# Gate weights of the two best experts from one tanh instead of a softmax over eight

## The chip, the cores and the metric

The kernel runs on one core of a Trainium2 chip. A core has five engines, each with its own instruction stream: TensorE (PE in the profile; its weight loads are PEld), VectorE (DVE), ScalarE (ACT), GpSimd (POOL) and SyncE (SP, which here only starts DMAs). They meet through semaphores. The metric is the device time of one execution in microseconds; lower is better.

## The reference

The input has 16 batches of 768 tokens with 128 channels. Each batch goes through attention with eight heads, then through a mixture of eight experts of which every token uses two weights:

```
logits = x @ Wg                                   # eight per token
probs = softmax(logits)
top_p, _ = top_k(probs, 2)
top_p = top_p / sum(top_p)                        # two weights per token
for i in range(2):
    h = gelu(einsum(x * top_p[..., i:i+1], W1) + b1)   # all eight experts
    out = out + einsum(h, W2) + b2_sum
```

Every expert is computed for both weights; only the weights come from the gate. After the renormalisation the two weights are e1/(e1+e2) and e2/(e1+e2), with e1 and e2 the exponentials of the two largest logits.

## The kernel before

Everything is fp32. One round works on one batch. The feed-forward part of a round is 64 "units" (two chunks of 384 tokens, eight experts, four column blocks). The attention part of the next batch is cut into steps, and a table (PLAN) says in which of the 64 slots each step is issued, so that attention of batch b+1 runs between the units of batch b. In slot k each engine issues the attention steps of that slot, then unit k+4, then on TensorE the second product of unit k. There are 15 such rounds in a loop and one last round without a following batch; the attention of batch 0 stands ahead of the loop by itself.

A unit goes: TensorE forms z in PSUM in three products (lines 901 to 903, function `unit`); VectorE multiplies z by the ratio of the two weights into h1 (line 735); ScalarE applies gelu to z and to h1 (lines 540 and 541); GpSimd adds the two into hsum (line 453); TensorE multiplies hsum by W2 (line 912). TensorE's z has two buffers: unit m waits (line 897) until the gelu of line 540 of unit m-2 is done.

The end of the attention part prepares the expert input of the next batch, in slots 50 to 60:

- stats, seed, root, scale: layer norm on VectorE; line 627 is one of its small instructions, line 648 the six multiplies that form xn.
- turn (slot 56), gate (slot 57): TensorE transposes xn and forms the logits (line 879). VectorE takes the eight sorted logits of each of six token tiles (line 691) and subtracts the largest (line 694); ScalarE applies exp (line 524).
- weigh (slot 58): VectorE makes the two weights (`top`) and their ratio in eight instructions on 6 to 48 elements (lines 698 to 707), each waiting for the one before, and then scales xn by the larger weight in six multiplies of 128x128 (line 709).
- split (slot 60): TensorE transposes xn and the ratio (lines 886, 887); ScalarE and VectorE make x0_hi, ratio_b and x0_lo (lines 531, 532, 714). Unit 64, which is the first unit of the next batch, waits on TensorE for line 714.

In the gate slot ScalarE issues the gate's activation between the gelus of unit 60 and those of unit 61. After slots 58 and 59 VectorE goes on with the layer norm of the batch after next (lines 619 to 648). On ScalarE a table load (ACT_TABLE_LOAD) stands ahead of an activation whose function is not in the table set that is loaded.

Of the kernel before, what the change touches and what calls it, by code (L numbers as in the profile page):

```python
# [1 line left out]

# [7 lines left out]
ALU = mybir.AluOpType  # L24
ACT = mybir.ActivationFunctionType
AX = mybir.AxisListType

P = 128
# [60 lines left out]
WPB = len(WIDE) // 2  # L89
NPB = len(NARROW)  # L90

VCHAIN = 2 * (5 + 3 * NEWTON) + 7
NH1 = 4


# [20 lines left out]
def build(nc, x, Wq, Wk, Wv, Wo, time_bias, part_bias, Wg, W1, b1, W2, b2, out):  # L116
    with ExitStack() as ctx:
# [6 lines left out]
        def sem(name):  # L124
# [37 lines left out]
        ln_i = sb("ln_i", [P, TILES], I32)  # L162
        ln_y = sb("ln_y", [P, TILES])
        ln_t = sb("ln_t", [P, TILES])
        sorted_l, shifted, gate_e = (halves[:, 3, QCOLS + 48 * n:QCOLS + 48 * (n + 1)].rearrange(
            "p (i e) -> p i e", e=EXPERTS) for n in range(3))
        gate_s = sb("gate_s", [P, TILES, 4])
        probs = sb("probs", [P, TILES, 2])
        top = sb("top", [P, TILES, 2])
        ratio = sb("ratio", [P, TILES, 2])  # L170

# [305 lines left out]
        def _(act):  # L477
# [7 lines left out]
            def attention(r, step, a):  # L485
                if step in WIDE_STEPS:
                    s, _, filled = wide_at(r, step, a)
                    w = wide[s]
                if step == "turn":
                    act.wait_ge(wide_filled[s], filled)  # L490
                    act.copy(act_t[:, :], w[:, 0:TOK]).then_inc(wide_free[s], 1)
                elif step in ("query", "key"):
                    n, scale = (0, HD ** -0.5) if step == "query" else (2, 1.0)
                    act.wait_ge(wide_filled[s], filled)
                    act.activation(halves[:, n, :].bitcast(F32R), w[:, 0:TOK], ACT.Copy, scale=scale).then_inc(high_ready, 1)
                elif step == "value":
                    act.wait_ge(wide_filled[s], filled)
                    act.copy(val[:, :, :, 0:HD], w[:, 0:TOK].rearrange("p (i h d) -> p i h d", h=HEADS, d=HD)
                             ).then_inc(wide_free[s], 1)
                elif step == "rows":  # L500
                    act.wait_ge(wide_filled[s], filled)
                    act.activation(max_rows[:, 0, :].bitcast(F32R), w[0:GH * TILES, 0:P], ACT.Copy,
                                   scale=-1.0).then_inc(rows_high, 1)
                elif step == "scores":
                    g, hh, part = a
                    act.wait_ge(wide_filled[s], filled)
                    if not (g == 0 and isinstance(r.b, int) and r.b == 0) and hh == 0 and part == 0:

                        n = NARROW["mix", (1 - g, 1)]
                        act.wait_ge(narrow_filled, r.at(NPB, n + 1 - (NPB if g == 0 else 0)))  # L510
                    z0, z1 = ((0, 896), (896, 1664), (1664, ZW))[part]
                    act.activation(z[:, hh, z0:z1], w[:, 0:z1 - z0], ACT.Exp).then_inc(wide_free[s], 1)  # L512
                elif step == "mix":
                    g, qc = a
                    n = NARROW[step, a]
                    cols = QCOLS if qc == 0 else TOK - QCOLS
                    act.wait_ge(narrow_filled, r.at(NPB, n + 1))
                    if g == 1:

                        act.wait_ge(*taken(r, "divide", 0))  # L520
                    act.copy(mixed[:, qc * QCOLS:qc * QCOLS + cols], narrow[:, 0:cols]).then_inc(narrow_free, 1)  # L521
                elif step == "gate":
                    act.wait_ge(gate_shifted, r.at(1, 1))
                    act.activation(gate_e[:, :, :], shifted[:, :, :], ACT.Exp).then_inc(gate_exped, 1)
                elif step == "split":
                    act.wait_ge(wide_filled[s], filled)
                    if not (isinstance(r.b, int) and r.b == 0):

                        act.wait_ge(z_filled, r.at(UNITS, (a + 1) * UNITS_PER_CHUNK - UNITS))
                        act.wait_ge(z1_ready, r.at(UNITS, (a + 1) * UNITS_PER_CHUNK - UNITS + 2))  # L530
                    act.copy(x0_hi[:, a * CT:(a + 1) * CT], w[:, 0:CT]).then_inc(split_high, 1)
                    act.copy(ratio_b[:, a * CT:(a + 1) * CT], w[:, 512:512 + CT]).then_inc(split_high, 1)
# [28 lines left out]
        def _(vec):  # L561
# [37 lines left out]
            def attention(r, step, a):  # L599
# [72 lines left out]
                elif step == "sums":  # L672
                    vec.wait_ge(wide_filled[s], filled)
                    vec.reciprocal(recip[:, :, :], w[:, 0:TILES * GH].rearrange("p (i g) -> p i g", g=GH)).then_inc(wide_free[s], 1)
                elif step == "divide":
                    vec.wait_ge(wide_filled[s], filled)
                    if a == 1:

                        for hh in range(GH):
                            vec.wait_ge(stack_loaded[hh], r.at(2 * 4 * 16, 2 * 4 * 16))  # L680
                    vec.tensor_tensor(mixed_n[a][:, 0:TOK], mixed[:, :], w[:, 0:TOK], ALU.mult).then_inc(wide_free[s], 1)
                elif step == "project":
                    vec.wait_ge(wide_filled[s], filled)
                    vec.tensor_tensor(xs[:, :, :], w[:, 0:TOK].rearrange("p (i c) -> p i c", c=C),
                                      x_in[:, :, :], ALU.add).then_inc(wide_free[s], 1)
                elif step == "gate":
                    n = NARROW[step, a]
                    vec.wait_ge(narrow_filled, r.at(NPB, n + 1))
                    vec.sem_inc(vec_met, 1)
                    for i in range(TILES):  # L690
                        ins = vec.max(sorted_l[:, i, :], narrow[:, i * EXPERTS:(i + 1) * EXPERTS])
                    ins.then_inc(narrow_free, 1)
                    vec.wait_ge(narrow_free, r.at(NPB, n + 1))
                    vec.tensor_tensor(shifted[:, :, :], sorted_l[:, :, :], window(sorted_l[:, 0, :], 0, [[EXPERTS, TILES], [0, EXPERTS]]),
                                      ALU.subtract).then_inc(gate_shifted, 1)
                elif step == "weigh":
                    vec.wait_ge(gate_exped, r.at(1, 1))
                    vec.wait_ge(vec_chain, link(vec.tensor_reduce(gate_s[:, :, 0], gate_e[:, :, :], AX.X, ALU.add)))
                    vec.wait_ge(vec_chain, link(vec.reciprocal(gate_s[:, :, 1], gate_s[:, :, 0])))
                    vec.wait_ge(vec_chain, link(vec.tensor_tensor(probs[:, :, :], gate_e[:, :, 0:2],  # L700
                                                                  window(gate_s[:, 0, :], 1, [[4, TILES], [0, 2]]), ALU.mult)))
                    vec.wait_ge(vec_chain, link(vec.tensor_reduce(gate_s[:, :, 2], probs[:, :, :], AX.X, ALU.add)))
                    vec.wait_ge(vec_chain, link(vec.reciprocal(gate_s[:, :, 3], gate_s[:, :, 2])))
                    vec.wait_ge(vec_chain, link(vec.tensor_tensor(top[:, :, :], probs[:, :, :],
                                                                  window(gate_s[:, 0, :], 3, [[4, TILES], [0, 2]]), ALU.mult)))
                    vec.wait_ge(vec_chain, link(vec.reciprocal(ratio[:, :, 0], top[:, :, 0])))
                    vec.tensor_tensor(ratio[:, :, 1], top[:, :, 1], ratio[:, :, 0], ALU.mult)
                    for i in range(TILES):
                        ins = vec.tensor_scalar(xn[:, i, :], xn[:, i, :], top[:, i, 0:1], None, ALU.mult)
                    ins.then_inc(xn_ready, 1)  # L710
                    assert chain[0] == VCHAIN
                elif step == "split":
                    vec.wait_ge(split_high, r.at(4, 2 * a + 2))
                    ins = vec.tensor_tensor(x0_lo[:, a * CT:(a + 1) * CT], w[:, 0:CT], x0_hi[:, a * CT:(a + 1) * CT],
                                            ALU.subtract)
                    ins.then_inc(wide_free[s], 1)
                    if not (isinstance(r.b, int) and r.b == 0) and a == 0:
                        vec.wait_ge(out_ready, r.at(CHUNKS, 1 - CHUNKS + 1))
                    if a == 0:
                        residual(r, 0)  # L720
                    elif isinstance(r.b, int) and r.b == 0:
                        residual(r, 1)
# [219 lines left out]
```

## Time and profile before

| what | value |
|---|---|
| median of three timed executions | 2823.3 us (2819.64 to 2824.63) |
| span of the profiled execution, first to last instruction | 2817.5 us |
| what lies around the span (median less span) | 5.8 us |
| TensorE busy | 2460.9 us (87%) |
| weight loads busy | 2132.1 us (76%) |
| VectorE busy | 1485.6 us (53%) |
| ScalarE busy | 1694.7 us (60%) |
| GpSimd busy | 1087.3 us (39%) |
| mean granted clock of TensorE | 0.965 |

The profile gives the span of the profiled execution; its time from outside was not recorded apart, so the median of the timed ones stands for it. Busy shares are means over stages with different limits. In timelines a row begins with its start in microseconds and its length; "x6" merges six instructions, and "[0.97 <-ACT h L540]" is idle time of that engine just before, with what ended it.

### The profile page before, as it was taken

Reading aid. Unit: us, or ns where it says so; the run is one execution under the profiler, and the core shown is the slowest. Engines: PE = TensorE matmul, PEld = TensorE weight load, DVE = VectorE, ACT = ScalarE, POOL = GpSimd, SP = SyncE. Lnnn points to the kernel's source line nnn. Section 1 sums busy time; section 2 is a strip of 40 time slices with the busy share of each in tenths; the row PEclk is TensorE's granted clock in tenths of the full one; section 3 lists DMA queues with packets and bytes.
Section 4 is the critical chain, followed back from the end, with each engine's and each line's share of the span. In section 5 each row is a group of like instructions: output and inputs, shape, how many; then the busy total and the mean of one; then the engine's idle time right before and its main releaser. Section 6 shows DMA issues by size and latency. Waiting matters only on the chain.

```text
span 2817.5 us, 57193 instructions
## 1 busy us (share of the span) xinstructions
PE 2460.9 (87%) x18611; PEld 2132.1 (76%) x18611; DVE 1485.6 (53%) x4157; ACT 1694.7 (60%) x2788; POOL 1087.3 (39%) x1054
## 2 busy tenths in 40 slices
PE   1658989899998989989899898989989898998989
PEld 0447778787877878877787777878877787877879
DVE  7545375445636554474554636544573555547454
ACT  2126666665665666556566665666566566656667
POOL 6014244343424434343343424333343433434337
PEclk9679999999999999999999999999999999999999
DMA  2412121030212203021030212103021120302100
GB/s 32 71 37 29 22 33 27 10 47 10 27 27 30 29 7 49 6 32 27 12 46 9 29 25 32 27 8 48 10 27 27 25 35 7 43 11 32 27 9 7
DMA packets 62290, 73.55 MB, mean 26 GB/s; under 512 B 15936, under 2 KB 43488, under 8 KB 61920
## 3 DMA queue, kind: packets, MB, share of 16 engines
q1 hardware_dynamic: 62016, 69.89, 17.1%
q8 instruction: 173, 2.83, 0.4%
q14 instruction: 101, 0.83, 0.1%
HBM read 11.19 MB, written 6.29 MB: 6 GB/s over the span
## 4 chain that ended last, share of the span: by engine, by line
PE 65%; DVE 12%; issue 10%; ACT 8%; DMA 2%; POOL 1%; SPq 1%; DVEq 0%; POOLq 0%; ACTq 0%
PE acc L912 17%; PE zps L901 8%; PE wide L819 7%; PE narrow L852 5%; PE wide L835 5%; ACT z L512 5%; PE zps L902 5%; PE zps L903 5%; PE wide L838 4%; PE wide L866 2%; PE wide L873 2%; DVE wide L664 1%; DVE h L735 1%; PE wide L859 1%; DMA stack<-halves 1%
## 5 line engine op out<-in xcount | busy, mean ns | idle before, releaser
L453 POOL TENSOR_TENSOR hsum<-h 128x384 f32<-128x384 f32 x1024 | 1027.6, 1007 | 1575.0 <-ACT h L541 1507.3
L540 ACT ACTIVATE h<-zps,b_col 128x384 f32<-128x384 f32 x1024 | 594.2, 580 | 751.6 <-DVE h L735 728.3
L735 DVE TENSOR_TENSOR h<-zps,ratio_b 128x384 f32<-128x384 f32 x1024 | 562.1, 554 | 910.1 <-PE zps L903 906.1
L912 PE MATMUL acc<-w,hsum 128*128 128x128 f32 x6144 | 863.0, 277 | 1.4 <-DVE outt L744 1.2
L912 PEld LDWEIGHTS acc<-w,hsum 128*128 128x128 f32 x6144 | 845.8, 194 | 2.2 <-POOL hsum L453 1.7
L541 ACT ACTIVATE h<-h,b_col 128x384 f32<-128x384 f32 x1024 | 620.4, 606 | 0.0
L901 PE MATMUL zps<-x_hi,w_lo 128*128 128x384 f32 x1024 | 449.8, 439 | 105.8 <-ACT h L540 64.0
L664 DVE CUSTOM_DVE_ANT_0 wide<-wide,query_table 128x768 f32<-128x768 f32 (+5 forms) x768 | 463.0, 651 | 123.1 <-PE wide L819 117.3
L835 PE MATMUL wide<-stack 128*128 128x256 f32 (+3 forms) x1280 | 364.7, 317 | 71.8 <-ACT z L512 33.6
L512 ACT ACTIVATE z<-wide 128x896 f32<-128x896 f32 (+2 forms) x384 | 344.8, 918 | 87.3 <-PE wide L838 86.8
L902 PE MATMUL zps<-x_lo,w_hi 128*128 128x384 f32 x1024 | 352.5, 344 | 0.0
L903 PE MATMUL zps<-x_hi,w_hi 128*128 128x384 f32 x1024 | 351.7, 343 | 0.0
L901 PEld LDWEIGHTS zps<-x_hi,w_lo 128*128 128x128 f32 x1024 | 197.4, 193 | 191.8 <-issue 100.3
L838 PE MATMUL wide<-bias_rows,key_hot 128*128 128x256 f32 (+3 forms) x1280 | 340.5, 300 | 0.0
L835 PEld LDWEIGHTS wide<-stack 128*128 128x128 f32 x1280 | 244.9, 191 | 124.9 <-ACT z L512 77.6
L819 PE MATMUL wide<-stack 64*128 64x512 f32 (+3 forms) x1024 | 260.8, 364 | 17.2 <-DVE maxes L664 8.6
L838 PEld LDWEIGHTS wide<-bias_rows,key_hot 128*128 128x128 f32 x1280 | 245.8, 192 | 6.4
L819 PEld LDWEIGHTS wide<-stack 64*128 64x128 f32 x1024 | 164.0, 191 | 76.7 <-DVE maxes L664 13.4
L902 PEld LDWEIGHTS zps<-x_lo,w_hi 128*128 128x128 f32 x1024 | 199.4, 195 | 0.4
L903 PEld LDWEIGHTS zps<-x_hi,w_hi 128*128 128x128 f32 x1024 | 196.8, 192 | 0.0
L852 PE MATMUL narrow<-z,val 128*32 128x256 f32 (+3 forms) x2560 | 175.9, 393 | 3.5 <-ACT mixed L521 1.4
L852 PEld LDWEIGHTS narrow<-z,val 128*32 128x32 f32 x2560 | 83.0, 109 | 87.5 <-issue 21.8
(110 smaller groups left out, 1611.8 us busy)
## 6 DMA issues: line engine op xcount, KB each, us to landing
stack<-halves SPq DMA_DIRECT2D x512, 96.0 KB, 3.6
x_in<-in_x SPq DMA_DIRECT2D x136, 48.0 KB, 2.4
out_dram<-outt SPq DMA_DIRECT2D x256, 24.0 KB, 1.6
z<-in_L_ffn_W SPq DMA_DIRECT2D x8, 256.0 KB, 4.2
stack<-max_rows SPq DMA_DIRECT2D x64, 12.0 KB
bias_rows<-w_hi SPq DMA_DIRECT2D x1, 192.0 KB
bias_rows<-w SPq DMA_DIRECT2D x1, 192.0 KB
bias_rows<-w_lo SPq DMA_DIRECT2D x1, 192.0 KB
```

Of the source, the lines that this page charges most:

```text
L453: pool.tensor_tensor(hsum[:, m % NHS, :], h0[:, m % 2, :], h1[:, m % NH1, :], ALU.add).then_inc(hsum_ready, 1)
L540: act.activation(h0[:, m % 2, :], zps[m % 2][:, 0:CT], ACT.Gelu, bias=b1_col[:, j:j + 1]).then_inc(h0_ready, 1)
L541: act.activation(h1[:, m % NH1, :], h1[:, m % NH1, :], ACT.Gelu, bias=b1_col[:, j:j + 1]).then_inc(h1_ready, 1)
L664: ins = vec.tensor_tensor_reduce(w[:, at:at + n], w[:, at:at + n], query_table[:, h, TOK - n:TOK], 1.0, -3e38, ALU.add, ALU.max, maxes[:, ...
L735: vec.tensor_tensor(h1[:, m % NH1, :], zps[m % 2][:, 0:CT], ratio_b[:, c * CT:(c + 1) * CT], ALU.mult).then_inc(z1_ready, 1)
L819: ins = pe.matmul(w[:, at:at + k1 - k0], qst[0:64, hh, i * P:(i + 1) * P], kst[0:64, hh, k0:k1], start=True, stop=True)
L835: pe.matmul(w[:, at:at + q1 - q0], kst[:, hh, i * P:(i + 1) * P], qst[:, hh, q0:q1], start=True, stop=False)
L838: ins = pe.matmul(w[:, at:at + q1 - q0], key_hot[:, g, :], bias_rows[:, hh, q0 - i * P:q1 - i * P], start=False, stop=True)
L901: pe.matmul(zp, lo, x0_hi[:, cols], start=True, stop=False)
L902: pe.matmul(zp, hi, x0_lo[:, cols], start=False, stop=False)
L903: pe.matmul(zp, hi, x0_hi[:, cols], start=False, stop=True).then_inc(z_filled, 1)
L912: ins = pe.matmul(acc[:, n * P:(n + 1) * P], hsum[:, k % NHS, n * P:(n + 1) * P], w2[:, j, :], start=(j == 0 and n == 0), stop=(j == UNITS ...
```

## The change

The subtraction of the gate step now forms only d, the second logit taken from the first (one value per token, 6 per partition). ScalarE computes t = tanh(d/2). VectorE forms the weights as (1+t)/2 and (1-t)/2, then the reciprocal of the first and the ratio. Three small buffers are new, four are gone, and the count of chained VectorE instructions per round (VCHAIN) is five lower. The lines of the new kernel carry numbers that are 14 lower up to line 680 and 21 lower after the weigh step.

```diff
-VCHAIN = 2 * (5 + 3 * NEWTON) + 7
+VCHAIN = 2 * (5 + 3 * NEWTON) + 2
@@ buffers
-        sorted_l, shifted, gate_e = (halves[:, 3, QCOLS + 48 * n:QCOLS + 48 * (n + 1)].rearrange(
-            "p (i e) -> p i e", e=EXPERTS) for n in range(3))
-        gate_s = sb("gate_s", [P, TILES, 4])
-        probs = sb("probs", [P, TILES, 2])
+        sorted_l = halves[:, 3, QCOLS:QCOLS + 48].rearrange("p (i e) -> p i e", e=EXPERTS)
+        gate_d = sb("gate_d", [P, TILES])
+        gate_t = sb("gate_t", [P, TILES])
+        gate_r = sb("gate_r", [P, TILES])
@@ ScalarE, gate
-                    act.activation(gate_e[:, :, :], shifted[:, :, :], ACT.Exp).then_inc(gate_exped, 1)
+                    act.activation(gate_t[:, :], gate_d[:, :], ACT.Tanh, scale=0.5).then_inc(gate_exped, 1)
@@ VectorE, gate
-                    vec.tensor_tensor(shifted[:, :, :], sorted_l[:, :, :], window(sorted_l[:, 0, :], 0, [[EXPERTS, TILES], [0, EXPERTS]]),
-                                      ALU.subtract).then_inc(gate_shifted, 1)
+                    vec.tensor_tensor(gate_d[:, :], sorted_l[:, :, 0], sorted_l[:, :, 1], ALU.subtract).then_inc(gate_shifted, 1)
@@ VectorE, weigh
-                    vec.wait_ge(vec_chain, link(vec.tensor_reduce(gate_s[:, :, 0], gate_e[:, :, :], AX.X, ALU.add)))
-                    vec.wait_ge(vec_chain, link(vec.reciprocal(gate_s[:, :, 1], gate_s[:, :, 0])))
-                    vec.wait_ge(vec_chain, link(vec.tensor_tensor(probs[:, :, :], gate_e[:, :, 0:2],
-                                                                  window(gate_s[:, 0, :], 1, [[4, TILES], [0, 2]]), ALU.mult)))
-                    vec.wait_ge(vec_chain, link(vec.tensor_reduce(gate_s[:, :, 2], probs[:, :, :], AX.X, ALU.add)))
-                    vec.wait_ge(vec_chain, link(vec.reciprocal(gate_s[:, :, 3], gate_s[:, :, 2])))
-                    vec.wait_ge(vec_chain, link(vec.tensor_tensor(top[:, :, :], probs[:, :, :],
-                                                                  window(gate_s[:, 0, :], 3, [[4, TILES], [0, 2]]), ALU.mult)))
-                    vec.wait_ge(vec_chain, link(vec.reciprocal(ratio[:, :, 0], top[:, :, 0])))
-                    vec.tensor_tensor(ratio[:, :, 1], top[:, :, 1], ratio[:, :, 0], ALU.mult)
+                    vec.tensor_scalar(top[:, :, 1], gate_t[:, :], -0.5, 0.5, ALU.mult, ALU.add)
+                    vec.wait_ge(vec_chain, link(vec.tensor_scalar(top[:, :, 0], gate_t[:, :], 0.5, 0.5, ALU.mult, ALU.add)))
+                    vec.wait_ge(vec_chain, link(vec.reciprocal(gate_r[:, :], top[:, :, 0])))
+                    vec.tensor_tensor(ratio[:, :, 1], top[:, :, 1], gate_r[:, :], ALU.mult)
```

ScalarE in the loop, from the gelus of unit 60 to those of unit 61 (line 540 and 541), before the change; line 524 is the gate's activation:

```order
L540 ACTIVATE h<-zps,b_col 128x384
L541 ACTIVATE h<-h,b_col 128x384
L523 REGISTER_ALU
L524 ACT_TABLE_LOAD
L524 ACTIVATE halves<-halves 128x48
L537 REGISTER_ALU
L540 ACT_TABLE_LOAD
L540 ACTIVATE h<-zps,b_col 128x384
L541 ACTIVATE h<-h,b_col 128x384
```

The same place after the change, where the gelus are lines 526 and 527 and the gate's activation is line 510:

```order
L526 ACTIVATE h<-zps,b_col 128x384
L527 ACTIVATE h<-h,b_col 128x384
L509 REGISTER_ALU
L510 ACTIVATE gate_t<-gate_d 128x6
L523 REGISTER_ALU
L526 ACTIVATE h<-zps,b_col 128x384
L527 ACTIVATE h<-h,b_col 128x384
```

Two table loads are gone, one ahead of the gate's activation and one ahead of the gelu behind it; no other instruction of ScalarE moved. In the attention of batch 0, ahead of the loop, no table load stood at line 524, and none is gone there.

VectorE in the loop, from the gate's subtraction to the six multiplies, before the change (register instructions left out; line 735 is unit 61):

```order
L694 TENSOR_TENSOR halves<-halves 128x48
L735 TENSOR_TENSOR h<-zps,ratio_b 128x384
L698 TENSOR_REDUCE gate_s<-halves 128x6
L699 RECIPROCAL gate_s<-gate_s 128x6
L700 TENSOR_TENSOR probs<-halves,gate_s 128x12
L702 TENSOR_REDUCE gate_s<-probs 128x6
L703 RECIPROCAL gate_s<-gate_s 128x6
L704 TENSOR_TENSOR top<-probs,gate_s 128x12
L706 RECIPROCAL ratio<-top 128x6
L707 TENSOR_TENSOR ratio<-top,ratio 128x6
L709 TENSOR_SCALAR xn<-xn,top 128x128 x6
```

And after it (line 714 is unit 61, line 688 the six multiplies):

```order
L680 TENSOR_TENSOR gate_d<-halves 128x6
L714 TENSOR_TENSOR h<-zps,ratio_b 128x384
L683 TENSOR_SCALAR top<-gate_t 128x6
L684 TENSOR_SCALAR top<-gate_t 128x6
L685 RECIPROCAL gate_r<-top 128x6
L686 TENSOR_TENSOR ratio<-top,gate_r 128x6
L688 TENSOR_SCALAR xn<-xn,top 128x128 x6
```

Eight small instructions became four, in the same place of the stream. TensorE, GpSimd and SyncE have the same instructions in the same order as before.

## Rows read from the trace of the kernel before

**Rows 1.** The page: span and the busiest engine (busy us, share, instructions).
```profile
span 2817.5 us, 57193 instructions
PE 2460.9 (87%) x18611; PEld 2132.1 (76%) x18611; DVE 1485.6 (53%) x4157; ACT 1694.7 (60%) x2788; POOL 1087.3 (39%) x1054
```

**Rows 2.** Groups by line, ScalarE's table loads: count | busy us, mean ns | idle before.
```profile
L540 ACT ACT_TABLE_LOAD x46 | 59.0, 1283 | 24.3 <-DVE h L735 22.1
...
L524 ACT ACT_TABLE_LOAD x15 | 19.2, 1283 | 0.3
```

**Rows 3.** Waits, whole span: engine line waited for: us, times, longest.
```profile
ACT h L540 <- DVE h L735: 728.3, 591, 3.0
...
PE zps L901 <- ACT h L540: 64.0, 59, 8.4
...
PE zps L901 <- DVE x_lo L714: 41.8, 16, 2.8
```

**Rows 4.** Timeline of ScalarE around the last gate in the loop.
```profile
2718.21 0.60 ACT L541 ACTIVATE h<-h,b_col 128x384 f32<-128x384 f32 x1
2718.83 1.28 ACT L524 ACT_TABLE_LOAD   x1
2720.12 0.24 ACT L524 ACTIVATE halves<-halves 128x48 f32<-128x48 f32 x1
2720.61 1.28 ACT L540 ACT_TABLE_LOAD   x1 [0.24 <-DVE h L735]
2721.90 0.58 ACT L540 ACTIVATE h<-zps,b_col 128x384 f32<-128x384 f32 x1
```

**Rows 5.** Timeline of VectorE, same place.
```profile
2719.80 0.21 DVE L694 TENSOR_TENSOR halves<-halves 128x48 f32<-128x48 f32 x1
2719.97 0.56 DVE L735 TENSOR_TENSOR h<-zps,ratio_b 128x384 f32<-128x384 f32 x1
2720.45 0.20 DVE L698 TENSOR_REDUCE gate_s<-halves 128x6 f32<-128x48 f32 x1
...
2722.05 1.26 DVE L709 TENSOR_SCALAR xn<-xn,top 128x128 f32<-128x128 f32 x6
2723.23 1.02 DVE L735 TENSOR_TENSOR h<-zps,ratio_b 128x384 f32<-128x384 f32 x2
...
2726.10 0.93 DVE L627 TENSOR_SCALAR ln_v<-moments 128x6 f32<-128x6 f32 x1
```

**Rows 6.** Timeline of TensorE: units 63, 64 and 67.
```profile
2722.54 0.45 PE L901 MATMUL zps<-x_hi,w_lo 128*128 128x384 f32 x1 [0.97 <-ACT h L540]
...
2728.06 0.44 PE L901 MATMUL zps<-x_hi,w_lo 128*128 128x384 f32 x1 [2.75 <-DVE x_lo L714]
...
2733.21 0.44 PE L901 MATMUL zps<-x_hi,w_lo 128*128 128x384 f32 x1 [1.31 <-ACT h L540]
```

**Rows 7.** Timeline of GpSimd, same round.
```profile
2713.02 2.07 POOL L453 TENSOR_TENSOR hsum<-h 128x384 f32<-128x384 f32 x2 [0.63 <-ACT h L541]
...
2723.07 1.10 POOL L453 TENSOR_TENSOR hsum<-h 128x384 f32<-128x384 f32 x1 [3.17 <-ACT h L541]
2725.03 1.97 POOL L453 TENSOR_TENSOR hsum<-h 128x384 f32<-128x384 f32 x2 [0.86 <-ACT h L541]
```

**Rows 8.** Timeline of VectorE: line 648 ahead of the loop, and in the loop.
```profile
192.71 1.62 DVE L648 TENSOR_SCALAR xn<-xs,moments,ln_y 128x128 f32<-128x128 f32 x6
...
2712.18 3.00 DVE L648 TENSOR_SCALAR xn<-xs,moments,ln_y 128x128 f32<-128x128 f32 x6
```

**Rows 9.** Timeline of VectorE: batch 0's gate, ahead of the loop.
```profile
204.18 3.83 DVE L700 TENSOR_TENSOR probs<-halves,gate_s 128x12 f32<-128x12 f32 x1
...
208.98 1.26 DVE L709 TENSOR_SCALAR xn<-xn,top 128x128 f32<-128x128 f32 x6
```

**Rows 10.** Busy time from unit 64's start, two rounds: start:end length, engines (instructions), granted clock.
```profile
1555.30:1558.70 3.40, 3.34 (x13) 3.35 (x14) 2.71 (x11) 1.08 (x2) 0.27 (x1) 0.53 0.00 0
2728.00:2731.40 3.40, 3.34 (x24) 3.34 (x25) 3.14 (x11) 1.08 (x2) 0.70 (x1) 1.00 0.00 0
```

## Prediction

> **What bounds the kernel now.** I read the page first: TensorE is busy for 87% of 2817.5 us [rows 1], so a gain must come from TensorE's gaps, not from the busy time of the engine that is changed. Next the groups of ScalarE: 61 table loads at lines 524 and 540, 1283 ns each [rows 2]. Fifteen of them stand ahead of the gate's exp, and 15 of the 46 ahead of the gelu behind it; the code shown ahead says that these 30 go. They cost ScalarE 30 x 1.283 = 38.5 us. Then the waits: ScalarE itself waits 728 us for VectorE's line 735, so it has room; TensorE waits 64.0 us for ScalarE's gelu and 41.8 us for VectorE's x_lo, the latter 16 times, once a batch [rows 3]. So the question is which of the two is late at the gate.
>
> The timelines of the last gate in the loop answer it; all rounds of the loop look alike here, so one is worked out and multiplied by 15. ScalarE ends unit 60 at 2718.81, loads a table, runs exp at 2720.12, loads again at 2720.61 and starts unit 61's gelu at 2721.90 [rows 4]. TensorE misses that gelu: unit 63 starts at 2722.54 after a gap of 0.97. But its next stop is unit 64 at 2728.06, after a gap of 2.75 that VectorE's x_lo ends [rows 6]. VectorE has no gap between: subtraction 2719.80, unit 61 at 2719.97, the eight small instructions from 2720.45, the six multiplies from 2722.05, units 62 and 63 from 2723.23, then the next layer norm up to the split [rows 5]. A wait that is removed on TensorE before 2722.54 is therefore only moved into the gap before 2728.06. VectorE's chain bounds this place, and ScalarE's loads are beside it.
>
> **The change part by part.** All times are those of the round above.
>
> Table loads: exp's load covered the wait for the logits, and its successor can go at once. Without the second load unit 61's gelu starts at 2720.61, when its input is there, 1.29 earlier [rows 4]. TensorE's unit 63 moves up by its gap, 0.97, and waits at the split instead. Worth on the path: nothing.
>
> Tanh for exp: the input is ready when the subtraction ends, 2720.01; exp took 0.24 for 48 elements, and the new one has 6. It ends by 2720.3, before VectorE asks at 2720.45. Nothing on the path.
>
> Subtraction, 6 elements for 48: by rows 5, 0.56 for 384 elements and 0.21 for 48, an element costs about 1 ns, so 0.04 is saved. All that follows on VectorE moves by it.
>
> Weigh: eight instructions took 2722.05 - 2720.45 = 1.60, or 0.20 each. Of the four new ones the second does not wait for the first, and the multiplies don't wait for the fourth, as now. I count three steps, 0.60: a saving of 1.00. Bounds: four full steps, saving 0.80; and two and a half, 1.10.
>
> What takes it back: the six multiplies now start at 2721.05, and GpSimd's sum comes earlier too, because the gelu does. GpSimd's sum of unit 61 starts 1.17 after the gelu of line 540 (2723.07 less 2721.90 [rows 4, 7]); it will ask at 2721.78. The multiplies start every 0.20 (1.18 to the next unit, by six [rows 5]), so the fifth starts at 2721.84 and meets it. What such a meeting costs: the tiny line 627 at 2726.10 took 0.93 and ended at 2727.03, just after GpSimd's pair that ended at 2727.00; line 648 took 1.62 ahead of the loop where GpSimd was idle, and 3.00 in the loop beside a pair of sums [rows 5, 7, 8]. A multiply that meets a running sum stands until its end. Today the sum starts at 2723.07 during the sixth multiply, so GpSimd is the one that stands, 0.1. With a sum of 1.10 from 2721.78 the fifth multiply ends at about 2722.91 instead of 2722.12: 0.79 lost. Of 1.00 there remain 0.21. If the fifth gets in ahead of the sum, the sixth stands instead, with about the same result. Bounds: all of it lost, or nothing of it.
>
> [...]
>
> Behind the multiplies everything follows VectorE rigidly: units 62 and 63, their gelus, the pair of sums at 2725.03, line 627 that stands for that pair, x_lo, unit 64. So a round saves 0.04 + 0.21 = 0.25, and 15 rounds 3.75.
>
> Batch 0, ahead of the loop: line 700 stands until 208.01 for GpSimd's work on the weights, and the multiplies start at 208.98 [rows 9], 0.97 later. After the change the first small instruction will stand in its place until the same moment, and about 0.55 follow. Saves 0.4, once.
>
> Sum against the profiled execution: 2817.5 - 4.15 = 2813.4 of span, and with the 5.8 between span and median, 2823.3 - 4.15 = 2819.2. I forecast 2819.
>
> **The rivals.**
>
> First, the meeting does not happen or costs little: the multiplies slip past the sum. For it: the fifth and sixth multiply start within 0.25 of the sum, and my steps are good to 0.1 or so. Against: the whole chain is rigid and would have to be 0.25 faster. Price 1.04 a round, 15.6 + 0.4 = 16.0: 2807.
>
> Second, the other side: TensorE's clock. Today its idle time here is in two pieces, 0.97 and 2.75, with work between; after the change the first closes and the gap before unit 64 grows to some 3.2 to 3.5. [...] Against: two thirds of the idle time exists already, and most rounds keep the high clock here.
>
> Third, the loads stay, as the change doesn't do what it says. [...] The order of instructions shows none. Then the sum would come late as today and miss the multiplies, while unit 63 at 2722.54 would hold VectorE's second line 735, which could start about 0.8 later, 2723.3 instead of 2723.70: 0.4 a round, 2817.
>
> Fourth, ScalarE bounds after all: 2 x 1.283 x 15 = 38.5, 2785. The gap of 2.75 that x_lo ends, not a gelu, speaks against it.
>
> Fifth, something behind gives back even the quarter (a DMA or the clock elsewhere): 2823.
>
> **How the numbers follow.** Chances: forecast 0.52, first rival 0.20, second 0.14, third 0.04, fourth 0.03, fifth 0.07. The likeliest case has its own range of 2814 to 2823, from a lost saving to twice mine with the scatter of the timed runs. The 8 in 10 range runs from the first rival to the near part of the second: 2807 to 2830. A measurement of this kernel tells 0.2%, 5.6 us, from no change. Faster than 2817.7: the first and fourth rival, half of the third, and a third of the forecast: 0.40. Slower than 2828.9: two thirds of the second: 0.09. Within: 0.51.
>
> **What would show it.** In the profile after: 31 table loads at these two lines for 61; the gelu of unit 61 about 0.8 after the subtraction's start, not 2.1; the six multiplies starting some 1.3 after it and lasting about 2.1 instead of 1.26, with a sum of GpSimd beginning in their middle; unit 64 about 8.0 after the subtraction instead of 8.26; TensorE's wait for x_lo near 50 us, and that for the gelu lower by about 14. I am wrong if the multiplies keep 1.26 (first rival), if the granted clock falls near unit 64 in most rounds (second), or if unit 64 moves by over a microsecond.

## The result and the profile after

The changed kernel took 2805.6 us (median of 4 runs, 2798.97 to 2806.65) against 2822.1 for the kernel before on the same chip; the ratio is 0.9934 with a 95% interval of 0.992 to 0.9949. I had forecast 2819, a gain of 0.15%, with a range from 2807 to 2830. The gain was four times as large. A "round" below is the time from one gate subtraction to the next, averaged over 14 rounds of the loop in the profiled execution; "low" is the lower of the two clocks that the profiles record for TensorE, 0.50 of full speed (the other is 1.00, and a row with a value between them spans both), and a "low stretch" is a stretch of a few microseconds in which that clock was granted. The "turn of the loop" is the jump from the end of the loop's body back to its start; TensorE's first products behind it start 16 to 18 us after the subtraction. Rounds are counted from the first one of the loop.

The page of the kernel after, its first and third line, answering to [rows 1]:

```profile
span 2803.3 us, 57024 instructions
...
PE 2461.5 (88%) x18611; PEld 2135.8 (76%) x18611; DVE 1478.3 (53%) x4093; ACT 1651.6 (59%) x2758; POOL 1087.5 (39%) x1054
```

TensorE's work is the same. ScalarE lost 43 us of busy time, and the span shrank by only 14, which speaks against loads on the path; e1 and the pair f2 and f3 below decide it. Its groups, for [rows 2] (line 526 was 540):

```profile
L526 ACT ACT_TABLE_LOAD x31 | 39.8, 1283 | 20.0 <-DVE h L714 18.0
```

The 30 loads are gone. The waits, for [rows 3] (880 was 901, 693 was 714):

```profile
ACT h L526 <- DVE h L714: 750.1, 601, 3.0
...
PE zps L880 <- DVE x_lo L693: 48.0, 16, 3.2
...
PE zps L880 <- ACT h L526: 37.0, 35, 8.1
```

TensorE's wait for the gelu fell by 27 us, that for x_lo rose by 6. I had forecast 14 for the first: the gap of 0.97 ahead of unit 63 is gone in every round, 14.6 us, and the gap of 1.3 ahead of unit 67 is down to between 0.0 and 0.4 in 13 rounds of 14, where before it was down in 4. Those are the rounds in which unit 64 runs at the low clock, as the table below shows. The last gate in the loop, ScalarE, VectorE, GpSimd and TensorE one after the other, for [rows 4 to 7]; its subtraction starts at 2706.14:

```profile
2706.34 0.21 ACT L510 ACTIVATE gate_t<-gate_d 128x6 f32<-128x6 f32 x1 [1.50 <-DVE gate_d L680]
2706.96 0.58 ACT L526 ACTIVATE h<-zps,b_col 128x384 f32<-128x384 f32 x1 [0.41 <-DVE h L714]
```

```profile
2706.85 0.17 DVE L684 TENSOR_SCALAR top<-gate_t 128x6 f32<-128x6 f32 x1
2707.05 0.19 DVE L685 RECIPROCAL gate_r<-top 128x6 f32<-128x6 f32 x1
2707.28 0.17 DVE L686 TENSOR_TENSOR ratio<-top,gate_r 128x6 f32<-128x6 f32 x1
2707.36 2.00 DVE L688 TENSOR_SCALAR xn<-xn,top 128x128 f32<-128x128 f32 x6
2709.28 1.01 DVE L714 TENSOR_TENSOR h<-zps,ratio_b 128x384 f32<-128x384 f32 x2
```

```profile
2708.12 1.16 POOL L439 TENSOR_TENSOR hsum<-h 128x384 f32<-128x384 f32 x1 [2.21 <-ACT h L527]
```

```profile
2714.11 0.44 PE L880 MATMUL zps<-x_hi,w_lo 128*128 128x384 f32 x1 [3.17 <-DVE x_lo L693]
```

This is the forecast's picture: gelu at 0.82 after the subtraction, multiplies from 1.22, GpSimd's sum starting at 1.98, six multiplies in 2.00 instead of 1.26, unit 64 at 7.97 where it was at 8.26. One by one, the fifth multiply started at 2.01, 0.02 behind the sum, and still took its usual 0.28, while the sum took 1.16 for 1.00; the sixth, due at 2.20, stood until the sum ended and took 1.02. A round of the loop should then have lost 0.28. It lost 1.08: from 167.47 to 166.39 us.

Where the rest is shows in the granted clock. Busy time in stretches of 3 us, from unit 64's start and from the next batch's first transposes behind the turn of the loop. The columns are those of [rows 10]: start:end and length, then TensorE, its weight loads, VectorE, ScalarE and GpSimd with their instructions, then the granted clock, the DMA share and GB/s. The kernel before, the fifth round, 167.53 us long:

```profile
1051.60:1054.60 3.00, 3.00 (x22) 3.00 (x23) 2.74 (x11) 1.08 (x2) 0.41 (x1) 1.00 0.00 0
1060.70:1063.70 3.00, 3.00 (x14) 3.00 (x15) 0.56 (x1) 0.80 (x1) 0.68 (x1) 0.50 0.21 41
```

The kernel after, its fifth round (165.11 us) and its eighth (168.06 us):

```profile
1048.10:1051.10 3.00, 3.00 (x15) 3.00 (x16) 2.75 (x11) 1.08 (x2) 0.46 (x1) 0.66 0.00 0
1057.10:1060.10 3.00, 3.00 (x24) 3.00 (x25) 0.62 (x2) 0.80 (x1) 0.72 (x1) 1.00 0.21 42
1547.70:1550.70 3.00, 3.00 (x12) 3.00 (x13) 2.23 (x10) 1.07 (x2) 0.00 (x0) 0.50 0.00 0
1557.60:1560.60 3.00, 2.93 (x13) 2.94 (x13) 0.40 (x1) 0.80 (x1) 0.37 (x1) 0.50 0.22 44
```

Before, the usual round has the high clock at unit 64 and the low one behind the turn: 14 products are at work in those 3 us, where the fifth round after has 24. After, the low clock has come to unit 64 in nearly every round, and in half of them the stretch behind the turn is at full speed. Counted in the clock's record over 14 rounds, with all later runs (unit 64's place is the median of the 14; the runs are explained in the next section):

| kernel | unit 64 after the subtraction | round | low at unit 64 | low behind the turn | median us | ratio (95%) |
|---|---|---|---|---|---|---|
| before | 8.26 | 167.47 | 4 | 12 | 2822.1 | |
| changed | 7.98 | 166.39 | 13 | 7 | 2805.6 | 0.9934 (0.992 to 0.9949) |
| e1, loads kept | 7.54 | 165.94 | 11 | 9 | 2796.0 | 0.9921 (0.9904 to 0.9937) |
| e2, loads gone alone | 8.93 | 167.46 | 8 | 7 | 2821.0 | 1.0011 (1.0001 to 1.0021) |
| e3, one step more | 8.21 | 166.98 | 11 | 7 | 2814.1 | 0.998 (0.997 to 0.999) |
| f1, before, filling that missed | 8.27 | 169.42 | 0 | 14 | 2846.6 | 1.0097 (1.0076 to 1.0118) |
| f2, changed, filling that missed | 8.01 | 168.92 | 0 | 14 | 2840.4 | 1.0077 (1.006 to 1.0093) |
| f3, e1, filling that missed | 7.55 | 168.40 | 0 | 14 | 2830.6 | 1.0043 (1.0026 to 1.006) |
| g1, before, filled at 64 | 8.27 | 167.94 | 0 | 14 | 2824.2 | 1.001 (1.0 to 1.0019) |
| g2, changed, filled at 64 | 7.99 | 167.19 | 0 | 14 | 2814.8 | 0.9978 (0.9968 to 0.9987) |
| h1, before, filled at both | 8.27 | 166.07 | 0 | 0 | 2802.0 | 0.993 (0.9912 to 0.9948) |
| h2, changed, filled at both | 8.01 | 165.62 | 0 | 0 | 2791.9 | 0.9893 (0.9876 to 0.9911) |
| v1, multiplies first | 6.93 | 164.96 | 14 | 5 | 2784.5 | 0.9881 (0.9865 to 0.9898) |
| v2, v1 filled at the turn | 6.93 | 164.45 | 8 | 0 | 2776.2 | 0.9842 (0.9826 to 0.9859) |
| v3, v1 filled at both | 6.93 | 164.41 | 0 | 0 | 2773.5 | 0.9834 (0.9817 to 0.985) |

All ratios are to the kernel before on the same chip, whose median there was 2818.8 to 2823.9; so medians from different chips compare to some 5 us only. Ahead of batch 0's gate, where the kernels don't differ, the profiled executions are already up to 3 us apart (199.7 to 202.7). The runs e1 to e3 shared a chip, and so did f1 to f3 with v1, g1 and g2 with v2 and v3, and h1 with h2. Low stretches elsewhere in the round are not counted here: the kernel before has one 160 us after the subtraction in 5 rounds, h1 one at 159 in 4, and these rounds are no longer than the others. One place where it did matter comes with e3.

### The profile page after: what moved, and what is told of

The parts are those of the page before. It is cut to its first block, busy times and chain, and to the rows that moved or that the text cites. A ratio compares the mean times of both kernels' runs of the same rounds, so it can differ in the third digit from the quotient of the medians.

```text
span 2803.3 us, 57024 instructions
## 1 busy us (share of the span) xinstructions
PE 2461.5 (88%) x18611; PEld 2135.8 (76%) x18611; DVE 1478.3 (53%) x4093; ACT 1651.6 (59%) x2758; POOL 1087.5 (39%) x1054
## 4 chain that ended last, share of the span: by engine, by line
PE 69%; DVE 11%; issue 10%; ACT 8%; POOL 1%; DMA 0%; DVEq 0%; SPq 0%; POOLq 0%; ACTq 0%
PE acc L891 19%; PE zps L880 8%; PE wide L798 7%; PE narrow L831 6%; PE zps L882 5%; PE zps L881 5%; ACT z L498 5%; PE wide L814 5%; PE wide L817 4%; PE wide L845 2%; PE wide L852 2%; DVE h L714 2%; DVE wide L650 1%; PE wide L838 1%; PE wide L782 1%
```

## The experiments

Three theories stood. Local: only VectorE's way to unit 64 counts, with the meeting of the multiplies and GpSimd's sum. Clock: the rest of the gain is the place of the low stretches. Loads: the table loads were on the path after all. Where an edit changes the number of chained VectorE instructions, the count VCHAIN follows; that line is left out of the diffs shown.

**e1, the loads kept.** Unit 61's gelu comes late again while the chain stays short.

```diff
-act.activation(gate_t[:, :], gate_d[:, :], ACT.Tanh, scale=0.5)
+act.activation(gate_t[:, :], gate_d[:, :], ACT.Exp, scale=0.5)
```

> The changed kernel with exp in the place of tanh, so the two table loads of each round come back while VectorE's short chain stays (the weights it computes are not those of the reference). Local theory (only VectorE's way to unit 64 counts, and GpSimd's sum meets the multiplies only when the loads are gone): the six multiplies last 1.26 again, unit 64 starts 7.8 to 7.9 after the subtraction instead of 8.26 before and 8.0 in the changed kernel; 15 x 0.4 + 0.4 = 6 us below before, ratio 0.998. Clock theory (most of the change's gain comes from where TensorE's clock falls, and that depends on how its idle time is cut up): TensorE's idle time is cut as before (a gap of about 1 and one of 2.3), so the low stretches stay where they were before and the ratio is 0.998 as well; if instead the gain is the same as that of the change, 0.993, then loads and idle pieces have nothing to do with it. Rival that the loads were on the path: ratio 1.00 or more.

Measured: 2796.0, ratio 0.9921. VectorE, GpSimd and TensorE at the last gate, whose subtraction starts at 2697.30:

```profile
2698.52 1.26 DVE L688 TENSOR_SCALAR xn<-xn,top 128x128 f32<-128x128 f32 x6
```

```profile
2700.56 1.98 POOL L439 TENSOR_TENSOR hsum<-h 128x384 f32<-128x384 f32 x2 [3.49 <-ACT h L527]
```

```profile
2704.84 0.43 PE L880 MATMUL zps<-x_hi,w_lo 128*128 128x384 f32 x1 [2.04 <-DVE x_lo L693]
```

The multiplies are done before the sum starts and last 1.26; unit 64 is at 7.54, better than the 7.8 expected. Two loads a round are back, and the kernel is no slower than the change: 0.9921 and 0.9934 have overlapping intervals, and the same pair with filling on one chip (f2 and f3 below) has the kernel with the loads ahead by 9.8 us. The loads theory fails, and the meeting is shown. The time went further down than 0.998, for which the clock's part was again not foreseen (9 rounds of 14 low behind the turn, not 12).

**e2, the loads gone alone.** The kernel before, with

```diff
-window(sorted_l[:, 0, :], 0, [[EXPERTS, TILES], [0, EXPERTS]])
+window(sorted_l[:, 0, :], 7, [[EXPERTS, TILES], [0, EXPERTS]])
-act.activation(gate_e[:, :, :], shifted[:, :, :], ACT.Exp)
+act.activation(gate_e[:, :, :], shifted[:, :, :], ACT.Tanh)
```

> The kernel before with tanh in the place of exp, so only the two table loads go and the eight small instructions stay (the subtraction takes the smallest logit, to keep the values finite; the weights are not those of the reference). Local theory: GpSimd's sum now asks 1.98 after the subtraction's start, just ahead of the first multiply at 2.25, so VectorE stands until about 3.0 and unit 64 starts at about 9.0 instead of 8.26: 15 x 0.75 = 11 us slower, ratio 1.004. Rival that the loads were on the path: faster by up to 38 us, ratio 0.986. Clock theory: the gap of 0.97 is closed and the gap ahead of unit 64 is the longest of all, above 4, so the clock is low at unit 64 in nearly every round and less often at the next batch's first transposes; that gives some 10 us back, ratio near 1.000.

Measured: 2821.0, ratio 1.0011. VectorE and TensorE at the last gate, whose subtraction starts at 2721.22; GpSimd's sum ran from 2723.21 to 2724.20:

```profile
2723.39 0.83 DVE L707 TENSOR_TENSOR ratio<-top,ratio 128x6 f32<-128x6 f32 x1
2724.15 1.25 DVE L709 TENSOR_SCALAR xn<-xn,top 128x128 f32<-128x128 f32 x6
```

```profile
2730.15 0.44 PE L901 MATMUL zps<-x_hi,w_lo 128*128 128x384 f32 x1 [3.17 <-DVE x_lo L714]
```

The last small instruction, with two inputs in SBUF, stood for the sum and took 0.83 where it took 0.17, and unit 64 came at 8.93, 0.67 late. By the local theory alone this is +10 us. The kernel was slower by 3; 7 rounds were low behind the turn where 12 had been. Both halves of the expectation hold: removing the loads does harm at its place, and the clock pays most of it back.

**e3, one step more.** The changed kernel with line 685 issued twice, each waiting for the one before.

```diff
+vec.wait_ge(vec_chain, link(vec.reciprocal(gate_r[:, :], top[:, :, 0])))
 vec.wait_ge(vec_chain, link(vec.reciprocal(gate_r[:, :], top[:, :, 0])))
```

> The changed kernel with the reciprocal of the weigh step issued twice, one more chained small instruction of 0.2 us. Local theory: the multiplies start 0.2 later, GpSimd's sum stands where it was, so the fourth or fifth multiply waits for the same end and the two behind it come as before or one multiply (0.2) later; unit 64 at 8.0 to 8.2 after the subtraction. If the local quarter of a microsecond were all of the gain the time would go back to the kernel before, ratio 0.999 to 1.000. Clock theory: TensorE's idle time is cut as in the changed kernel, and the ratio stays near 0.993 to 0.995.

Measured: 2814.1, ratio 0.998, between the two expectations. Unit 64 is at 8.21, all but where it was before the change, so locally almost nothing is gained; the round is still 0.49 shorter than before, with 7 low stretches behind the turn where 12 had been. The 0.23 that unit 64 lost against the change cost 8.5 us in the medians (12 when each is taken against the kernel before on its own chip), not 3.5.

Yet e3 has as many low stretches behind the turn as the change, and two fewer at unit 64, so the two columns of the table don't explain its loss. The trace does in part: in three of its rounds (169.1 to 169.8 us) a third low stretch stands 121 us after the subtraction, at the products of line 815, behind a wait for a DMA that lasted 2.0 to 2.2 in these rounds and 1.2 to 1.4 in the others. The third round, and then the twelfth, which has the same two low stretches without the third and took 167.34:

```profile
829.85 0.50 PE L815 MATMUL wide<-stack 128*128 128x512 f32 x1 [2.23 <-DMA stack<-max_rows]
...
2331.07 0.50 PE L815 MATMUL wide<-stack 128*128 128x512 f32 x1 [1.37 <-DMA stack<-max_rows]
```

```profile
830.60:833.90 3.30, 3.30 (x16) 3.30 (x16) 0.00 (x0) 1.73 (x2) 0.00 (x0) 0.50 0.00 0
2331.80:2335.10 3.30, 3.16 (x23) 2.71 (x21) 0.00 (x0) 2.66 (x4) 0.08 (x1) 1.00 0.00 0
```

The three rounds lie 2.1 above that one, 0.45 a round over the 14, of the 0.59 by which e3's round is above the change's. Why the DMA came later there is open. The place of the low stretches moves with small shifts, and no fixed price can be put on it.

**f1 to f3, a filling that missed.** Products that nobody reads, to keep TensorE at work in its two long idle stretches, in the kernel before, the changed one and e1:

```diff
+if j == 0 and c == 0 and not isinstance(r.b, int):      # ahead of unit 64
+    pe.wait_ge(narrow_free, r.at(NPB, NARROW["gate", 0] + 1))
+    for _ in range(3):
+        pe.matmul(narrow[:, 0:448], ident[:, :], W448, start=True, stop=True)
...
+if a == 0 and not isinstance(r.b, int):                  # in turn, ahead of its wait
+    for _ in range(2):
+        pe.matmul(w[:, 0:448], ident[:, :], W448, start=True, stop=True)
```

W448 stands for the first 448 columns of w2.

> The kernel before with TensorE kept at work in its two longest idle stretches of a round: three products of 448 columns ahead of its wait for unit 64, two ahead of its wait for the first transposes of the next batch, into PSUM that is overwritten; nothing reads them. Clock theory: the low stretches near unit 64 and at the next transposes go or become rare, a round takes about 165 us or less for 167.5, and the time falls by 20 us or more although work was added: ratio 0.990 or lower. Rival (the low clock costs nothing, it only lies in slack): ratio 1.000 to 1.003, as the added products can only delay.

> The changed kernel with the same added products. Local theory with the clock held alike: unit 64 is 0.28 earlier than in f1_before_filled, and the difference between the two is 15 x 0.28 + 0.4 = 4.6 us, not the 16 measured without the products. If the change itself is worth the 16, this run is 16 below f1.

> The kernel of e1_loads_kept (short chain, exp, both table loads) with the same added products. Local theory: unit 64 is 0.72 earlier than in f1_before_filled: 15 x 0.72 + 0.4 = 11 us below it, and 6.5 us below f2_changed_filled. If the clock made the difference between e1 and the change, the two are alike here.

Measured: 2846.6, 2840.4 and 2830.6, ratios 1.0097, 1.0077 and 1.0043. f1's expectation failed. The products in turn ran behind the idle stretch, not in it: the stretch of 2.4 us there ends at the first transposes of the loop's body and is put down to "issue", so it is the turn of the loop, not the wait in turn. All rounds kept the low clock behind the turn in all three, and the differences shrank towards the local ones: 6.2 between f1 and f2 (4.6 expected, 16.5 without filling) and 16.0 between f1 and f3 (11 expected, 22.8 without filling).

**g1 and g2, filled ahead of unit 64 alone**, the first half of that edit.

> The kernel before with the three added products ahead of unit 64 alone. (In f1 to f3 the two products meant for the next transposes ran behind the gap there, which is the turn of the loop, and only cost time.) Clock theory as it now stands: idle time ahead of unit 64 brings a low stretch there, which is cheap because much of it lies in slack and which takes the place of the dear one behind the turn of the loop. With the products no low stretch comes at unit 64 and one comes behind the loop's turn in every round: a round takes 167.3 to 167.6, ratio 0.999 to 1.001. If low stretches at unit 64 were a pure loss, taking them away would make it faster: 0.998 or less.

> The changed kernel with the three added products ahead of unit 64. Clock theory: nearly every round now has the low stretch behind the loop's turn, as in the kernel before, a round takes 0.28 less than in g1, 167.1 or so; 2815 to 2819, ratio 0.998, so that taking idle time from TensorE makes the changed kernel 10 us slower. If the 16 us of the change were its own, the ratio stays near 0.993.

Measured: 2824.2 (1.001) and 2814.8 (0.9978), both ratios as expected; g1's round, 167.94, is 0.3 longer than expected. No low stretch at unit 64, one behind the turn in every round, and the changed kernel is 9 us slower than without the products (11 against the kernel before on each one's chip), although they fit into idle time and unit 64 starts where it did. The cheap low stretch had stood in for the dear one.

**v1, the multiplies first.** The changed kernel, with a chain of two small instructions:

```diff
-vec.tensor_scalar(top[:, :, 1], gate_t[:, :], -0.5, 0.5, ALU.mult, ALU.add)
 vec.wait_ge(vec_chain, link(vec.tensor_scalar(top[:, :, 0], gate_t[:, :], 0.5, 0.5, ALU.mult, ALU.add)))
-vec.wait_ge(vec_chain, link(vec.reciprocal(gate_r[:, :], top[:, :, 0])))
-vec.tensor_tensor(ratio[:, :, 1], top[:, :, 1], gate_r[:, :], ALU.mult)
+vec.reciprocal(ratio[:, :, 1], top[:, :, 0])
...
-act.copy(ratio_b[:, a * CT:(a + 1) * CT], w[:, 512:512 + CT])
+act.activation(ratio_b[:, a * CT:(a + 1) * CT], w[:, 512:512 + CT], ACT.Copy, bias=-1.0)
```

> A version of the change whose multiplies get away ahead of GpSimd's sum: only the larger weight is made from tanh, its reciprocal is written in the ratio's place (ratio = 1/larger - 1), and ScalarE takes the 1 off where it copies ratio_b anyway. Two small VectorE instructions are left of eight. Local theory: the multiplies start at 0.94 to 1.0 after the subtraction and the sixth at about 1.95, before the sum asks at 1.99; they last 1.26, and unit 64 starts at about 7.0 to 7.3 for 8.26 before: 15 x 1.1 = 16 us from this alone, and the time is at or below that of e1_loads_kept (2796). If the sixth meets the sum all the same: unit 64 at 7.9, 2806. The clock adds or takes up to 12 in either case.

Measured: 2784.5, ratio 0.9881. VectorE, GpSimd and TensorE at the last gate, whose subtraction starts at 2685.69:

```profile
2686.34 0.16 DVE L683 TENSOR_SCALAR top<-gate_t 128x6 f32<-128x6 f32 x1
2686.54 0.19 DVE L684 RECIPROCAL ratio<-top 128x6 f32<-128x6 f32 x1
2686.64 1.22 DVE L686 TENSOR_SCALAR xn<-xn,top 128x128 f32<-128x128 f32 x6
2687.78 1.01 DVE L712 TENSOR_TENSOR h<-zps,ratio_b 128x384 f32<-128x384 f32 x2
```

```profile
2687.68 1.05 POOL L439 TENSOR_TENSOR hsum<-h 128x384 f32<-128x384 f32 x1 [2.20 <-ACT h L527]
```

```profile
2692.62 0.44 PE L878 MATMUL zps<-x_hi,w_lo 128*128 128x384 f32 x1 [2.66 <-DVE x_lo L691]
```

The sixth multiply starts at 1.90, 0.09 ahead of the sum, so GpSimd stands for 0.05 and VectorE not at all. Unit 64 is at 6.93: 1.33 a round, of which the change as made got 0.28.

**v2 and v3, v1 with filling at the turn, and at both places.** Two products at the end of the loop's body (v2), and two ahead of unit 64 as well (v3):

```diff
+if k == UNITS - 1 and not isinstance(r.b, int):
+    pe.wait_ge(narrow_free, r.at(NPB, NPB + NARROW["gate", 0] + 1))
+    for _ in range(2):
+        pe.matmul(narrow[:, 0:448], ident[:, :], W448, start=True, stop=True)
```

> v1 with two added products of 448 columns at the end of the loop's body, ahead of the gap at the loop's turn. If the gap of 2.3 is the fetch of the first instructions of the body and TensorE can work meanwhile, the products cost little and the low stretch behind the turn (5 of 14 rounds in v1) goes: 5 x 1.9 = 10 us below v1, 2775. If the engine has to end them first, each round is 1.2 longer and what the clock gives is lost: 2790 to 2803.

> v2 with two added products ahead of unit 64 as well. Clock theory: a round without any low stretch. If v2's products are free: under 2770. If they cost 1.2 a round: 2780 to 2795. More low stretches than in v1 would say that the added products don't count as work for the clock.

Measured: 2776.2 (0.9842) and 2773.5 (0.9834). TensorE at a turn of the loop in v2:

```profile
2528.09 1.67 PE L895 MATMUL narrow<-w,ident 128*128 128x448 f32 x4
2530.70 0.87 PE L775 MATMUL wide<-ident,xn 128*128 128x128 f32 x6 [0.94 <-issue]
```

The engine worked 1.67 us of the turn and stood idle for 0.94 (0.9 to 1.4 over v2's rounds); the kernel before stood 2.39 at its turn in the fifth round. The products are almost free, and no round was low behind the turn any more. v2 met its expectation (2775); v3 missed its "under 2770", as a low stretch at unit 64 is cheap. Most of it lies in the gap ahead of unit 67, which in v2 was 1.3 in each round without one and 0.0 to 0.4 in each round with one; in v2 rounds with one took 164.61 on average (8), and rounds without one 164.22 (6). v3's fifth round, the same two places as above, both at the high clock:

```profile
1039.20:1042.20 3.00, 2.99 (x21) 3.00 (x22) 2.74 (x11) 1.08 (x2) 0.36 (x1) 1.00 0.00 0
1048.60:1051.60 3.00, 2.98 (x23) 2.99 (x24) 0.91 (x2) 1.29 (x3) 0.43 (x1) 1.00 0.17 33
```

v3 is the fastest version that was run, 1.7% below the kernel before; v1 needs no added work and is 1.2% below it.

**h1 and h2, both kernels filled at both places**, three products ahead of unit 64 and two at the turn.

> The kernel before with three added products ahead of unit 64 and two ahead of the loop's turn, as v3. Clock theory: neither of the two low stretches is left, and rounds differ from those of v3 only by where unit 64 starts (8.26 against 6.93): 164.4 + 1.33 = 165.7 a round, 2773.5 + 15 x 1.33 + 0.5 = 2794, ratio 0.990. If the two low stretches were not what made the kernel before slow, it stays above 2810.

> The changed kernel with the same added products. With the clock high in both kernels the change is worth its own part only, 15 x 0.28 + 0.4 = 4.6 us: 2789, 0.16% below h1. If the change's 16 us were its own and not the clock's, this run is 16 below h1, 2778.

Measured: 2802.0 (0.993) and 2791.9 (0.9893). Neither has a low stretch at the two places in any round. Filling alone makes the kernel before 0.7% faster, about as much as the change did. Between the two, the change is worth 10.1 us in the medians and 0.45 a round (6.8 us in 15): more than my 4.6, less than the 16.5 without filling. Both expected medians were too low, by 8 and 3.

## Why the prediction was wrong

Local steps. The loads off the path, right: TensorE got its 0.97 and waited longer at x_lo, and e1, with the loads, is no slower than the change. Tanh hidden, right: 0.21 us, ended before VectorE asked. The chain, right: 1.03 shorter to the multiplies' start, forecast 1.04. The meeting with GpSimd, right: 0.74 lost, forecast 0.79; the fifth multiply got in and the sixth stood, the variant that the forecast named with the same result. Unit 64 came 0.28 earlier, forecast 0.25. Batch 0's multiplies came 0.56 earlier after their subtraction, forecast 0.4. The 5.8 between span and median is not what lies around the span: for one and the same execution of the changed kernel that is 1.8 (2805.14 less 2803.3), so the profiled execution of the kernel before was itself some 4 us faster than its median. The forecast difference doesn't rest on it. A small instruction with two SBUF inputs stood for a sum as well: in e2 line 707 took 0.83, where it took 0.17 in the kernel before.

What failed is one step: "So a round saves 0.04 + 0.21 = 0.25, and 15 rounds 3.75", with "all rounds of the loop look alike here" behind it. It takes the other 157 us of a round as fixed; the measured saving was 1.08 a round. They are not fixed: a round with the low clock behind the turn of the loop is longer than one without. In the changed kernel the rounds with a low stretch at unit 64 alone took 165.49 on average (7 rounds), those with one at both places 167.37 (6): 1.9. Taking all of these stretches away took 1.6 a round off from g2 to h2 and 1.9 from g1 to h1. The change went from 12 to 7 such stretches in 14 rounds, 8 to 10 us by these prices.

The first rival's number, 2807, is close to the 2805.6 measured by luck: its sign, multiplies that keep 1.26, did not come (2.00). The second rival, TensorE's clock, was right in what happens and had the wrong sign. It had the gap before unit 64 grow and the low clock come there, as a loss. Both came: 3.17 us of idle where there had been 2.75, and 13 low rounds where there had been 4; with the gap filled (g1 and g2) there was none. The upper end of the range, 2830, rests on a price for this rival that was an estimate of mine and that no run shows; what v2 showed is about 0.4 a round, as most of it lies in the slack ahead of unit 67. What I did not ask is where the low stretch had been that it replaced. The rows for that were in the trace before: the first transposes behind the turn of the loop at half speed in 12 rounds of 14, and none of the three views I read shows it, as the engine counts as busy there.

How much is whose. Three pairs hold the clock's places alike in both kernels: the change is worth 6.2 us between f1 and f2 and 9.4 between g1 and g2 (all rounds low behind the turn), and 10.1 between h1 and h2 (none). So of the measured 16.5 us some 6 to 10 are its own, and the rest came from the clock, which g2 (9 us slower with idle time removed) and h1 (0.7% faster) show from both sides.

That own part is more than the 4.6 us of unit 64, and the waits show one more piece that the prediction lacked. In h1, at unit 76 in every second round, TensorE waits for a DMA into `stack`:

```profile
PE wide L819 <- DMA stack<-halves: 2.1, 8, 0.3
```

The row is there with 2.1 to 2.3 us in all five kernels with the old gate (before, e2, f1, g1, h1) and in none of the ten with the new one. The lead of h2 over h1 grows by 0.18 between units 72 and 80, where it lies, and so do v3's lead over h1 and g2's over g1. Why the old gate has this wait no run isolates.

Open are the other pieces. The lead of h2 over h1 is 0.27 at units 64 to 67, 0.09 behind the turn (units 68 to 72), 0.26 at unit 80 and 0.42 at unit 120; between h1 and v3 the round shrinks by 1.66 where unit 64 explains 1.33. And which rounds will be low behind the turn, or elsewhere as in e3, I cannot work out beforehand. Medians of this kernel are the sum of a small sure part and a part that depends on this.

## What to carry to other kernels

Before a saving is multiplied by the number of rounds, look at TensorE's granted clock round by round, in stretches of a few microseconds behind each of its idle stretches; a change of a quarter of a microsecond can move where it runs at half speed (here 0.28 at unit 64, and low behind the turn in 7 rounds of 14 where 12 had been). An engine that is released earlier starts its next instruction earlier, and on VectorE and GpSimd that instruction may now meet one of the other engine: give each edit both partners' start times, as here, where two dropped table loads by themselves made unit 64 0.67 us later. When small instructions stand ahead of large ones, issue first what the large ones need, and move the rest behind or onto an engine that touches the data anyway.

## What the runs showed of the hardware

- In the kernel before, ScalarE had a table load of 1.283 us at each of its 91 changes between exp and gelu (lines 512, 524 and 540). In the changed kernel none stood at the 30 changes between gelu and tanh in the loop, nor between exp and tanh in the attention of batch 0, where the load came with the first gelu as before.
- The turn of the loop leaves TensorE idle for 2.5 us on average in the kernel before (2.0 to 2.9), and matrix products queued ahead of it still run in that time: 1.67 us of them left 0.94 idle.
- Idle time removed from TensorE can make a kernel slower (g2, 9 us), and idle time filled with products that nobody reads can make it faster (h1, 0.7%; v2 against v1, 8 us on two chips).
- In a meeting of VectorE and GpSimd tenths of a microsecond decide who stands. A multiply that started 0.09 ahead of the sum (v1) or 0.02 behind it (the changed kernel) took its usual 0.28, and the sum took 1.05 and 1.16 for 1.00; one that was due 0.22 behind the sum stood 0.74.
